# A selective state-space block with a routed mixture of experts: where the low weight parts are made, and a new slot rule

## The reference, cut to what matters

```python
x = x + tanh(g_xattn) * ssm(ctx, layernorm(x))     # conv, silu, selective scan of 16 states, gate
x = x + tanh(g_ffn) * moe(layernorm(x))

def moe(x):                                        # x: 1024 x 256
    logits = x @ gate_w                            # 256 x 8
    top_logits, top_idx = top_k(logits, 2)
    top_w = softmax(top_logits)
    cw = zeros(1024, 8) with top_w at top_idx
    for e in range(8):
        h = silu(x @ w0[e]) * (x @ w1[e])          # 256 x 512 each
        out += cw[:, e] * (h @ wo[e])              # 512 x 256
    return out
```

## Time and profile before

| | |
|---|---|
| median of 3 runs | 297.42 us (296.88 to 297.59) |
| the profiled execution | 296.67 us, of which 294.8 us is the span of the trace |
| mean granted clock of TensorE | 0.98 |
| busy, share of the span | PE 89%, DVE 77%, ACT 64%, POOL 61% |
| L1055, gate and up products, mean of one recorded instruction of the first group | 436 ns |
| L405, a low part on GpSimd | 22 of them, mean 1294 ns |
| L1356, a low part on VectorE | 6 of them, mean 678 ns |
| L438, a gather on GpSimd | 23 of them, mean 1160 ns |
| L452, an accumulating store on GpSimd | 23 of them, mean 1585 ns |

### The profile page before, as it was taken

How to read it: one execution, slowest core, us unless ns; L and a number is a source line. 1 busy time by engine, 2 the same in 40 slices (tenths; PEclk the granted TensorE clock), 3 DMA queues, 4 the chain that set the end, 5 groups by cost and what they waited for, 6 DMA issues and landing times.

```text
span 294.8 us, 4705 instructions
## 1 busy us (share of the span) xinstructions
PE 262.5 (89%) x1170; PEld 176.4 (60%) x1171; DVE 227.1 (77%) x397; ACT 187.9 (64%) x348; POOL 179.4 (61%) x162
## 2 busy tenths in 40 slices
PE   7995597899789898887889989999999999999970
PEld 7432242334335354533467658989898989898960
DVE  2889989999999998999967877665665666565640
ACT  2895758775775657778497646565657575757540
POOL 6013278999999898999870231547464646465342
PEclk9999799999999999999988999999999999999996
DMA  7699400000000001000089420333333333333312
GB/s 239 215 390 387 152 2 0 1 0 0 0 1 2 1 0 71 0 2 1 0 280 333 176 68 19 44 65 46 63 42 65 43 64 50 57 53 53 39 21 32
DMA packets 16659, 22.70 MB, mean 77 GB/s; under 512 B 2554, under 2 KB 10274, under 8 KB 16642
## 3 DMA queue, kind: packets, MB, share of 16 engines
q1 hardware_dynamic: 11456, 16.41, 15.9%
q0 software_dynamic: 4416, 6.03, 13.0%
q10 hardware_dynamic: 770, 0.06, 0.2%
HBM read 17.38 MB, written 5.11 MB: 76 GB/s over the span
## 4 chain that ended last, share of the span: by engine, by line
PE 63%; DVE 15%; issue 11%; POOL 6%; ACT 3%; POOLq 1%; DVEq 0%; ACTq 0%
PE PZ L1091 11%; PE PU L1055 11%; PE PD L1055 11%; PE PY L860 8%; DVE states L1256 5%; POOL hC L414 5%; PE PY L1077 4%; DVE states L1262 3%; PE PZ L1046 2%; PE PZ L912 2%; PE PY L855 1%; PE PU L768 1%; PE PD L805 1%; DVE W_lo L1356 1%; PE PU L846 1%
## 5 line engine op out<-in xcount | busy, mean ns | idle before, releaser
L414 POOL TENSOR_TENSOR hC<-states,WO 128x512 f32<-128x512 f32 x63 | 79.9, 1280 | 15.4 <-PE PY L860 10.3
L1262 DVE TENSOR_TENSOR_SCAN states<-PD,states 128x512 f32<-128x512 f32 x64 | 77.6, 1213 | 1.1 <-ACT PD L625 0.9
L860 PE MATMUL PY<-hC,ident 128*128 128x512 f32 x128 | 67.7, 612 | 4.2 <-POOL hC L414 4.1
L452 POOL DMA_INDIRECT out<-lg,y_at x23 | 36.5, 1585 | 49.3 <-ACT lg L734 41.9
L625 ACT ACTIVATE PD<-WO,Aneg 128x510 f32<-128x510 f32 x64 | 43.9, 689 | 18.4 <-DVE states L1262 15.2
L1256 DVE TENSOR_TENSOR states<-PU,WO 128x512 f32<-128x512 f32 x64 | 42.9, 672 | 1.3 <-POOL hC L414 1.0
L438 POOL DMA_INDIRECT hC<-x_rows,x_at x23 | 26.7, 1160 | 25.5 <-DMA x_rows<-u 15.0
L718 ACT ACTIVATE hidT_hi<-PY 128x512 fp32r<-128x512 f32 x23 | 13.8, 600 | 37.8 <-PE PY L1077 35.7
L1491 DVE TENSOR_TENSOR dA<-PU,dA 128x512 f32<-128x512 f32 x23 | 15.9, 692 | 28.4 <-PE PU L1055 28.4
L1503 DVE TENSOR_TENSOR WO_lo<-WO,WO_hi 128x512 fp32r<-128x512 f32 x46 | 29.7, 688 | 9.4 <-issue 9.3
L860 PEld LDWEIGHTS PY<-hC,ident 128*128 128x128 f32 x128 | 22.5, 191 | 16.6 <-POOL hC L414 11.2
(11 more groups left out here) (253 smaller groups left out, 504.3 us busy)
## 6 DMA issues: line engine op xcount, KB each, us to landing
W<-in_L_ffn_w SPq DMA_DIRECT2D x16, 512.0 KB, 10.9
WO<-in_L_ffn_wo SPq DMA_DIRECT2D x8, 512.0 KB, 6.3
xs<-in_x SPq DMA_DIRECT2D x2, 512.0 KB, 5.4
out<-xs SPq DMA_DIRECT2D x2, 512.0 KB, 3.2
x_rows<-u SPq DMA_DIRECT2D x2, 512.0 KB, 4.8
early<-in_ctx SPq DMA_DIRECT2D x1, 512.0 KB, 4.1
hC<-x_rows,x_at POOLq DMA_INDIRECT x23
out<-lg,y_at POOLq DMA_INDIRECT x23, 3.8
```

The costliest lines, as they stand in the source:

```text
L414: pool.tensor_tensor(hC[:, n % 2, :], states[:, n % RING, :], C_rep[:, pair % C_RING, :], ALU.mult).then_inc(hc_done, 1)
L452: pool.indirect_dma_start(out=out, out_offset=bass.IndirectOffsetOnAxis(ap=y_at[:, s:s + 1], axis=0), in_=y_tile[s % 2], in_offset=None, c ...
L860: pe.matmul(PY[:, h, :], ident[:, :], hC[:, n % 2, :], start=False, stop=(m == DS - 1)).then_inc(y_done, 1)
L1262: dve.tensor_tensor_scan(states[:, n % RING, :], DEC[n % 2], states[:, n % RING, :], 0.0, ALU.mult, ALU.add).then_inc(scan_done, 1)
```

## The change

- `places`: the first column of the comparison table `iota_k` is set to -1, so that a count of 0 also exceeds it: each expert gets at least one slot, and slot s never belongs to an expert above s.
- The 14 late low parts are all made by GpSimd (`LATE`): 4 behind the gathers for slots 0 to 3, and 2 behind each of the gathers for slots 4 to 8. TensorE waits for them at `gate` of slots 3 to 7 and `up` of slots 6 and 7. `low_part`, its four evictions on ScalarE and VectorE's six subtractions are gone.
- TensorE's products that nobody reads are now 4 ahead of the table of rows, 1 ahead of the table of weights, and 2 around the first `x_turn` (`SPINS`).
- Row blocks 4 and 5 (the third pair): `add_x(1, 0)` and ScalarE's `x2_out(2)` are gone; VectorE adds PSUM to `xs` (`residual`).
- The last rows are stored in two transfers (`store_pair`).
- Ahead of the steps, `gate(1)` stands before `hid_turn(0)`, and steps 1 to 7 are written out instead of looped.

```diff
-WARM = 1
-POOL_SPLITS = tuple(range(EARLY, EARLY + 4))
-PE_SPLITS = tuple(range(EARLY + 6, EARLY + 10))
-DVE_SPLITS = tuple(range(EARLY + 4, EARLY + 6)) + tuple(range(EARLY + 10, len(SPLITS)))
+LATE = tuple(range(EARLY, EARLY + 8)) + (28, 29, 26, 27, 30, 31)
+GATE_LOW, UP_LOW = {3: 2, 4: 4, 5: 6, 6: 8, 7: 12}, {6: 10, 7: 14}
+SPINS = (4, 1, 2)
...
+            def store_pair(b):
+                sp.wait_ge(xn_ok, 2 * b + 2)
+                sp.dma_start(x_rows[b * L:(b + 1) * L, :]..., xn[:, 2 * b:2 * b + 2, :]).then_inc(x_stored, 16)
             def store_x2(q):
-                sp.wait_ge(x2_ok, (q + 1) * QB)
+                sp.wait_ge(x2_ok, QB + q)
+                if q:
+                    sp.wait_ge(x2_dve, 1)
...
-            store_rows(1)
+            store_pair(2)
+            store_pair(3)
             store_x2(1)
...
+            pool.memset(iota_k[:, :, 0:1], -1.0).then_inc(consts, 1)
...
             times_C(DU_AT[1], NT - 1)
-            for i in POOL_SPLITS:
-                lower(i)
-            pool.wait_ge(x_stored, 16 * NQ)
+            pool.wait_ge(x_stored, 16 * (NQ + 1))
             pool.wait_ge(x_at_ok, 1)
             for s in range(4):
                 x_gather(s)
+            for i in LATE[:4]:
+                lower(i)
             pool.wait_ge(stored, 16 * NQ)
             pool.wait_ge(y_at_ok, 1)
             for s in range(SLOTS):
                 if s + 4 < SLOTS:
                     x_gather(s + 4)
+                for i in LATE[2 * s + 4:2 * s + 6]:
+                    lower(i)
                 if s:
                     pool.wait_ge(y_out[1 - s % 2], 16 * ((s + 1) // 2))
                 pool.wait_ge(y_sb, s + 1)
...
-            x2_out(2)
             x2_out(3)
...
-            for j in range(len(PE_SPLITS)):
-                act.wait_ge(W_lo_ps, j + 1)
-                act.activation(lo_part(PE_SPLITS[j]), SPLIT[j], ACT.Copy).then_inc(W_lo_act, 1)
...
-            add_x(1, 0)
+            pe.wait_ge(base_kept, 2)
             for r in range(QB):
                 add_gz(1, r)
...
-            for j in range(3):
-                low_part(j)
-            for _ in range(WARM):
-                pe.matmul(TABLE, ident[:, :], W1_hi[:, 0, 0, :].bitcast(F32), start=True, stop=True)
+            spin(SPINS[0])
...
-            low_part(3)
+            spin(SPINS[1])
...
                 pe.wait_ge(xT_ok, s + 1)
+                if isinstance(s, int) and s in GATE_LOW:
+                    pe.wait_ge(W_lo_pool, EARLY + GATE_LOW[s])
...
-            keep_busy(1)
+            spin(SPINS[2] // 2)
             x_turn(0, 0, 16)
-            keep_busy(1)
+            spin(SPINS[2] - SPINS[2] // 2)
...
             gate(0, 0, first)
             x_turn(1, 1, 16)
-            pe.wait_ge(W_lo_dve, len(DVE_SPLITS))
             up(0, 0, first)
-            step(0, 0, 32)
-            step(1, 1, 32)
-            with pe.Fori(0, (SLOTS - 5) // UNROLL) as t:
+            second = expert_of(1)
+            x_turn(2, 0, 32)
+            gate(1, 1, second)
+            hid_turn(0, 0)
+            up(1, 1, second)
+            down(0, 0)
+            for s in range(1, 2 + UNROLL):
+                step(s, s % 2, 16 * (s // 2 + 2))
+            with pe.Fori(1, (SLOTS - 5) // UNROLL) as t:
...
+            def residual():
+                dve.wait_ge(x2_ps, QB + 1)
+                rows = xs[:, QBLK:QBLK + 2, :].rearrange("p t d -> p (t d)")
+                dve.tensor_tensor(rows, PZ[0][:, :], rows, ALU.add).then_inc(x2_dve, 1)
...
+            residual()
             row_stats(1, 0)
             places()
...
-            lower(DVE_SPLITS[:2])
             dve.scalar_tensor_tensor(out=y_at[:, :], ...).then_inc(y_at_ok, 1)
-            lower(DVE_SPLITS[2:])
```

More of the change, by code:

```diff
@@ L238, in build @@
         TABLE = bank[3]
-        SPLIT = [bank[i] for i in (4, 0, 1, 7)]
         x_rows = nc.dram_tensor("x_rows", [TOK, DX], F32, kind="Internal").ap()
@@ L267, in build @@
             sem, ("route", "mask_ok", "rank_ps", "egap_ok", "slots_ok"))
-        W_hi_ok, W_lo_pool, W_lo_dve, xT_split = map(sem, ("W_hi_ok", "W_lo_pool", "W_lo_dve", "xT_split"))
-        W_lo_ps, W_lo_act, last_hc, mask_sum, count_ps = map(sem, ("W_lo_ps", "W_lo_act", "last_hc", "mask_sum", "count_ps"))
+        W_hi_ok, W_lo_pool, xT_split = map(sem, ("W_hi_ok", "W_lo_pool", "xT_split"))
+        x2_dve, last_hc, mask_sum, count_ps = map(sem, ("x2_dve", "last_hc", "mask_sum", "count_ps"))
         w_hi_ok, w_lo_ok = sem("w_hi_ok"), sem("w_lo_ok")
@@ L381, in _ @@
                       allow_small_or_imprecise_dtypes=True).then_inc(consts, 1)
+            pool.wait_ge(consts, 11)
+            pool.memset(iota_k[:, :, 0:1], -1.0).then_inc(consts, 1)
             pool.memset(eps_col[:, :], EPS).then_inc(eps_ok, 1)
@@ L919, in add_gz @@
                     for h in range(2):
-                        mm = pe.matmul(x2[:, l, h, :], z_cols[:, q * QBLK + 2 * r + h, l, :], scaled_id[:, :], start=False, stop=(l == 1 and h == 1))
+                        alone = q == 1 and r == 0
+                        mm = pe.matmul(x2[:, l, h, :], z_cols[:, q * QBLK + 2 * r + h, l, :], scaled_id[:, :],
+                                       start=alone, stop=(alone or (l == 1 and h == 1)))
                 mm.then_inc(x2_ps, 1)
@@ L995, in _, with spin @@
             through(ADD_NEXT_AT + 1, NT)
[L997 to L1002, removed]
+            def spin(times):
+                for _ in range(times):
+                    pe.matmul(PD[1][:, :], ident[:, :], W1_hi[:, 0, 0, :].bitcast(F32), start=True, stop=True)
             pe.wait_ge(scan_done, NT)
@@ L1033, in _ @@
             mm.then_inc(w_at_ps, 1)
[L1035 to L1039, removed]
             def x_turn(s, i, loaded):
@@ L1067, in up @@
                     pe.wait_ge(hid_ok, s - 1)
+                if isinstance(s, int) and s in UP_LOW:
+                    pe.wait_ge(W_lo_pool, EARLY + UP_LOW[s])
                 product(W1_hi, W1_lo, bank[2:4], i, expert, u_ps)
@@ L1107, in step @@
                 down(s, i)
-            keep_busy(1)
+            spin(SPINS[2] // 2)
             x_turn(0, 0, 16)
-            keep_busy(1)
+            spin(SPINS[2] - SPINS[2] // 2)
             pe.wait_ge(slots_ok, 1)
             first = expert_of(0)
-            pe.wait_ge(W_lo_pool, EARLY + len(POOL_SPLITS))
-            pe.wait_ge(W_lo_act, len(PE_SPLITS))
-            pe.wait_ge(W_lo_dve, 2)
+            pe.wait_ge(W_lo_pool, EARLY)
+            pe.wait_ge(W_hi_ok, len(SPLITS))
             gate(0, 0, first)
             x_turn(1, 1, 16)
-            pe.wait_ge(W_lo_dve, len(DVE_SPLITS))
             up(0, 0, first)
-            step(0, 0, 32)
-            step(1, 1, 32)
-            with pe.Fori(0, (SLOTS - 5) // UNROLL) as t:
+            second = expert_of(1)
[7 more added lines that the diff above has]
+            with pe.Fori(1, (SLOTS - 5) // UNROLL) as t:
                 for j in range(UNROLL):
@@ L1282, in row_stat @@
             def row_stat(i):
-                dve.wait_ge(x2_ok, i // 2 + 1)
+                if i // 2 == QB:
+                    dve.wait_ge(x2_dve, 1)
+                else:
+                    dve.wait_ge(x2_ok, i // 2 + 1 if i < QBLK else QB + 1)
                 dve.bn_stats(stats[:, 1, i, :], xs[:, i, :]).then_inc(stats2_ok, 1)
+            def residual():
+                dve.wait_ge(x2_ps, QB + 1)
+                rows = xs[:, QBLK:QBLK + 2, :].rearrange("p t d -> p (t d)")
+                dve.tensor_tensor(rows, PZ[0][:, :], rows, ALU.add).then_inc(x2_dve, 1)
             def row_stats(q, r):
@@ L1351, in chosen_two @@
                                        mask[:, :, :].rearrange("p e t -> p (e t)"), 0.0, ALU.mult, ALU.add).then_inc(mask_sum, 1)
[L1353 to L1356, removed]
             def rows_hot(j):
@@ L1368, in places @@
                 dve.wait_ge(count_ps, 1)
-                dve.wait_ge(consts, 16)
+                dve.wait_ge(consts, 17)
                 count = COUNT[:, 0:E].rearrange("p (e o) -> p e o", o=1).to_broadcast((P, E, NBLK))
```

3 lines of the change are left out of this document (2 added, 1 removed).

## The result

The changed kernel takes 301.96 us (median of 4 runs, 301.0 to 302.46) against 297.15 us of the kernel before in the same set: a ratio of 1.016, 95% interval [1.0123, 1.0197]. It is slower, and within the predicted range by 0.04, but not for the reason that carried the forecast of 298.9. The profiled execution took 302.46 us, of which 300.6 is the span; before it was 296.67 and 294.8.

What follows compares the result with a forecast made beforehand. TensorE bound the expert loop, a chain without single bound the routing stage. TensorE alone would reach tile 9's turn at 207.8, but GpSimd's queue makes it 212.0 against 210.53: 1.5 us later, 298.9 us, range 294.9 to 302.0.

Steps and rivals of the forecast that it cites:

- The early start: Routing stage: statistics start 0.75 earlier, x_at comes 1.45 earlier, and the first gather moves from 167.55 to about 166.1.
- rival 3: Last rows land as late as before, two transfers sharing the queue with x rows; start gains nothing: 300.3, chance 0.05.
- The first turn at 169.45, the second at 172.0: TensorE's first gathered tiles: first turn 169.45 against 170.95 before, second 172.0 against 173.93, 1.9 earlier.
- rival 2: TensorE's clock falls to 1.2 GHz around the thin tables, making turn, gate and gather 3 2.3 us later: 301.2, chance 0.23.
- VectorE's own delay, up to 1.1, hides in its 1.20: Expert loop: VectorE's delay from meeting GpSimd, up to 1.1 a step, hides in its 1.20 us wait for up products.
- From there to the fourth turn 6.5: TensorE from second to fourth turn: a turn 0.2, up(0) 1.39 and one step 4.88, from 172.0 to 178.5.
- GpSimd's pace: GpSimd's queue from gather 3 through five rounds, 5.66 each against TensorE's 4.88, to gather 9 decides turn 9 at 212.0.
- the meetings: Collisions of GpSimd's low parts with VectorE's two-input instructions: four taken, adding 1.8 us to GpSimd's queue.
- no wait of a turn for its gather: Sign against the forecast: TensorE's waits for gathers, expected from about tile 7 on, are absent in the changed profile.
- The sum: GpSimd's terms put the turn of tile 9 at 212.0 against 210.53 before, 1.5 us later, giving 298.9.

Runs made afterwards that it cites:

- e1: Changed kernel with one more unread TensorE product ahead of each of the two tables (SPINS 5, 2, 2): 299.22 us, 1.0063 of the kernel before.
- e2: Changed kernel without GpSimd's 14 late subtractions, those parts set to zero ahead of its first gather: 299.52 us, 1.0055 of the kernel before.
- e3: Changed kernel with the 14 late parts zeroed as in e2 and the extra unread products of e1: 296.1 us, 0.9966 of the kernel before.
- e9: e5 with one part moved to VectorE, GpSimd's other four one each in rounds 1 to 4, none in round 0: 293.7 us, 0.988 of before.
- e6: Kernel before with only VectorE's residual, the two stores and gate(1) ahead of hid_turn(0), late parts unmoved: 296.17 us, 0.9966 of before.
- e5: Changed kernel, three parts back on TensorE and ScalarE, GpSimd making six behind the scan and one in each of five rounds: 296.25 us, 0.9943.
- e7: Changed kernel with e1's unread products and a small memset ahead of each late part on GpSimd: 302.04 us in one run.
- e10: Changed kernel with e1's unread products, each late GpSimd part waiting until the one before is written: 301.57 us, 1.0134 of the kernel before.

## Why the prediction was right in its sign and wrong in its cause

- **The early start: right.** The statistics start at 156.82 and `x_at` at 165.20 (predicted 157.05 and 165.0), the last rows land in 2.6 to 2.8 (2.3 taken; the DMA engines weren't nearly idle there, as rival 3's argument had it, but at 0.40 to 0.49 between 162 and 166 of the kernel before), the first gather starts at 166.40 (166.1) and the weights' table at 166.91 (166.7).
- **"The first turn at 169.45, the second at 172.0": this step failed.** They came at 172.19 and 176.65. The forecast needed the full clock, and the clock fell at 166. Where it was kept (e1), the second turn is 16.06 behind the choice, against 172.0 - 156.09 = 15.91 predicted. The fall was rival 2, with a chance of 0.23 and 2.3 as its price; it cost 4.67 (after against e1), because the half speed held until 176. The price had 0.5 for the table and part of the gate beside the two unread products; the table lost 1.62 and the whole gate 1.61. e1, which grants the forecast its condition, took 299.22, and the forecast was 298.9. That is close by luck in part: e1's loop holds VectorE's lockout and a second fall of the clock, which the forecast didn't have.
- **"VectorE's own delay, up to 1.1, hides in its 1.20": failed.** The bound came from the one meeting in the earlier trace rows, where VectorE got in after one part. In the loop it got in only when GpSimd's run of parts had ended, so the first pair took 4.56, and 9.20 - 6.49 = 2.7 of that reached TensorE. The pairs of rounds 1 and 2 (3.92 and 3.85) cost it another 1.2. e2 and e3 (pairs 1.3, 6.49) and e9 (1.29, 6.50) show it.
- **"From there to the fourth turn 6.5": right** where the parts are out of the way (e2, e3, e6, e9).
- **GpSimd's pace: right in sum, wrong in its parts.** From gather 3 to gather 9 it took 213.49 - 177.30 = 36.19; 0.95 + 5.0 + 0.3 + 28.3 + 1.8 = 36.35 were predicted. But the meetings added nothing to the parts (1317 ns at most); instead stores took up to 1.86 in place of 1.59, two gathers 1.24 and 1.23 in place of 0.97, and in its first round GpSimd waited 1.03 for ScalarE. And it set no turn: gather 9 at 213.49 was in time for a TensorE that was late by itself. The prediction had named this, no wait of a turn for its gather, as the sign that it is wrong. With the clock kept at the start such waits come (e1: 0.20 and 0.71).
- **The sum.** Turn ten came at 216.32, 4.3 after the predicted 212.0: the second turn 4.65 late by the clock, and a loop of 39.67 against the predicted 40.0, which agrees only because VectorE's lockout stands where waits for gathers had been put. So that the time lies in the range is luck in part too: its upper end was set by rival 2's 301.2, whose price was half of what the fall cost.

The Trainium skill ("SBUF — State Buffer", Summary: rules for kernel authors) says that of a VectorE instruction with two SBUF inputs and a GpSimd instruction that reads SBUF the second to issue is fully blocked until the first finishes. The trace agrees that one of the two stands still (e5's part took its 1.30, and the pair ended 1.15 behind it). Which one isn't told by the starts in the profile: the pair of e5 began 0.52 ahead of the part and lost, and in e1 and e7 the blocked pair lost at each end of a part too, as long as the next part followed without a gap.

## What to carry to other kernels

Useful work that wide matrix products did in the gaps between thin ones also kept the clock here (1.00 in before, e5 and e9): before such work is moved to another engine, the clock of that stretch goes into the sum, with what comes behind it at half speed. Work that is moved to GpSimd is placed one instruction at a time in rounds where VectorE's result isn't awaited, never in a row beside VectorE's instructions with two SBUF inputs. And an engine that idles 2 us a step doesn't take 2.5 us of work without setting the pace, as e1 and e10 show.

## What the runs showed of the hardware

- Who wins at the end of a GpSimd instruction is not always the same. Behind the scan VectorE got in after one part, and the second part took 1716 ns, although more parts were queued; in the loop it lost at each end unless GpSimd paused (0.46 in e10). Why is open.
- A gather that began 0.14 into VectorE's pair took 1.42. In e3, where pair and gather begin within 0.01 of each other (187.88 and 187.89), the gather took 0.99 and the pair 1.34. The Trainium skill ("SBUF — State Buffer", Who interferes with whom) infers that such a pair leaves descriptor writing alone; the 1.42 speaks against it, the 0.99 does not.
- Of TensorE's clock: one wide product of 0.86 more ahead of each of two tables of 24 and 48 columns was the difference between 1.00 (e1) and 0.50, 1.2 GHz, from 167 to 176 (after); which of the two products matters wasn't tested. e5 and e9 kept the full clock by low parts in the same place. That the products of e1 keep it in every execution isn't shown: over the whole span the six runs in the ratio of e3, which has them too, had a mean granted clock of 0.957 to 0.983, and those of e2, without them, 0.952 to 0.964.
- The clock also fell in the loop, in e1 and e7, to 0.50 for some 3 us, behind TensorE's wait for VectorE's first pair (2.15 in e1). After the same wait it stayed at 1.00 in the changed kernel; what decides is open.
